# Token mixer of a small audio tower: spectral products with swapped operands, spectra turned through DRAM, inverse transforms in one row

## The reference

```python
B, T, C, HID, K, H = (8, 256, 128, 512, 31, 4)     # x here is (64, 125, 128)
w = jax.nn.softmax(logits, axis=-1)                # 31 taps for each token and head
y = jnp.einsum('bthk,btkhd->bthd', w, xg).reshape(Bq, Tq, Cq)
y = y.transpose(0, 2, 1) + bias[None, :, None]
z = jax.lax.conv_general_dilated(y, Wc, (1,), 'VALID', dimension_numbers=('NCH', 'OIH', 'NCH'))
z = z + bc[None, :, None]
z = jax.nn.selu(z.transpose(0, 2, 1))
return z @ W2.T + b2
```

## Time and profile before

| | us |
|---|---|
| median of three runs | 2085.88 (2084.6 to 2088.66) |
| the profiled execution | 2083.48 |
| its span in the trace | 2081.4 |
| the token mixer in it | 0 to 457.0 |
| its four chunks | 158.1 to 457.0 |
| PE busy, whole span | 1879.5 (90%) |

### The profile page before, as it was taken

One profiled execution on the slowest core, in us unless ns is written; L12 is line 12 of the kernel. 1 busy time (PEld: TensorE's weight loads), 2 busy tenths in 40 slices (PEclk: granted clock), 3 DMA queues, 4 the chain that ended last, 5 costly groups with the idle time before them and its releaser, 6 DMA issues. The chain is left out here.

```text
span 2081.4 us, 46638 instructions
## 1 busy us (share of the span) xinstructions
PE 1879.5 (90%) x16570; PEld 1313.2 (63%) x16570; DVE 1522.3 (73%) x3461; ACT 1257.5 (60%) x2263; POOL 968.1 (47%) x874
## 2 busy tenths in 40 slices
PE   5889999979999799999999999989999999958882
PEld 4678878855555456666666666556666666646771
DVE  5543464446888699999999999657778878867785
ACT  2444464455555377777777777667777777625771
POOL 0000000003454398888888887700344544565773
PEclk9999999999999899999999999999999999959996
DMA  8870010028990000000000000000000000036886
GB/s 295 324 274 20 23 42 11 1 61 361 413 397 5 12 11 11 11 10 10 10 10 10 10 10 10 20 11 2 2 16 19 12 15 20 13 90 194 227 226 209
DMA packets 87385, 178.52 MB, mean 86 GB/s; under 512 B 25917, under 2 KB 63214, under 8 KB 77846
## 3 DMA queue, kind: packets, MB, share of 16 engines
q1 hardware_dynamic: 78646, 160.11, 22.6%
q0 software_dynamic: 6624, 12.70, 1.8%
q10 hardware_dynamic: 1920, 3.11, 0.4%
HBM read 82.00 MB, written 94.86 MB: 85 GB/s over the span
## 5 line engine op out<-in xcount | busy, mean ns | idle before, releaser
L1154 ACT ACTIVATE b_pool_b<-b_pool_a,c_b 128x1024 f32<-128x1024 f32 x384 | 436.6, 1150 | 176.8 <-DVE b_pool_a L1390 154.2
L1227 POOL TENSOR_TENSOR b_pool_c<-b_pool_b 128x512 f32<-128x512 f32 x384 | 491.5, 1288 | 111.2 <-ACT b_pool_b L1154 61.7
L1390 DVE TENSOR_TENSOR b_pool_a<-b_p_s,c_shares 128x1024 f32<-128x1024 f32 x384 | 454.1, 1216 | 50.9 <-PE b_p_s L993 43.7
L991 PE MATMUL b_p_s<-c_x_hi,c_w_hi 128*128 128x512 f32 x384 | 296.3, 772 | 1.9 <-DVE b_pool_a L1390 1.9
L998 PE MATMUL b_p_y<-b_pool_c,c_w 128*128 128x512 f32 x384 | 196.7, 593 | 0.0
L998 PE MATMUL b_p_p<-b_pool_c,c_w 128*128 128x512 f32 x384 | 194.8, 591 | 0.0
L256 POOL COPY a_work<-a_vec 128x64 f32<-128x64 f32 x4 | 1.2, 304 | 378.3 <-PE a_p_A L347 224.6
L1279 DVE TENSOR_TENSOR b_pool_b<-b_p_s,b_decay 96x384 f32<-96x384 f32 x256 | 124.6, 546 | 41.6 <-PE b_p_s L862 41.3
L992 PE MATMUL b_p_s<-c_x_lo,c_w_hi 128*128 128x512 f32 x384 | 153.4, 399 | 0.0
L993 PE MATMUL b_p_s<-c_x_hi,c_w_lo 128*128 128x512 f32 x384 | 152.0, 396 | 0.0
L654 POOL TENSOR_TENSOR d_ln_rstd<-d_ln_var,d_ln_power 128x2 f32<-128x2 f32 x48 | 33.8, 704 | 250.1 <-DVE d_ln_var L650 250.1
(11 more groups left out here) (352 smaller groups left out, 4591.0 us busy)
## 6 DMA issues: line engine op xcount, KB each, us to landing
slots<-b_pool_c SPq DMA_DIRECT2D x55, 1040.0 KB, 25.4
e_wb<-e_weights SPq DMA_DIRECT2D x111, 164.0 KB
band_scratch<-a_work SPq DMA_DIRECT2D x16, 1024.0 KB, 5.6
a_work<-band_scratch SPq DMA_DIRECT2D x16, 1023.5 KB, 8.0
a_raw<-in_Wc SPq DMA_DIRECT2D x16, 512.0 KB, 3.8
e_xb<-slots SPq DMA_DIRECT2D x111, 65.0 KB
c_shares<-c_share_lists SPq DMA_DIRECT2D x12, 512.0 KB, 3.7
e_yb<-e_again SPq DMA_DIRECT2D x12, 512.0 KB, 6.1
```

The costliest lines, as they stand in the source:

```text
L991: nc.tensor.matmul(p_h[q % SLOTS][:, 0:WIDE], w1_hi[:, q, :], x_hi[s][:, :], start=True, stop=False)
L1154: nc.scalar.activation(hid[q % SLOTS][:, :, :], gelu_in[q % SLOTS][:, :, :], ACT.Gelu, bias=b1[:, q:q + 1]).then_inc(s_ge, 1)
L1227: nc.gpsimd.tensor_tensor(both[q % SLOTS][:, :], hid[q % SLOTS][:, 0, :], hid[q % SLOTS][:, 1, :], ALU.add).then_inc(s_bo, 1)
L1390: v.tensor_tensor(gelu_in[q % SLOTS][:, :, :], p_h[q % SLOTS][:, 0:WIDE].unsqueeze(1).to_broadcast([128, 2, WIDE]), shares[s][:, :, :], AL ...
```

## The change

- The two operands of the products are swapped: the piece of `R` is loaded as weights and the piece of `V` moves. A bank then holds (part, example) by (frequency, output channel). Number and size of the matmuls are as before; the first one has 64 columns of weights in place of 64 moving ones.
- The copies of a bank go to one of four buffers `zs[k % 4]`, 256 KB each, and SP writes it from there to a tensor in DRAM, `z_scratch` (two of them, chunks in turn), in pieces of 512 bytes. A copy waits until the write of the bank four earlier has landed.
- SP reads the tensor back by groups of 4 examples, 125 rows (coefficients) of 2 KB, into one of eight buffers `zt[k % 8]`. The first read of a chunk waits for all its writes; a read into a used buffer waits for the `to_time` that used it.
- `turn`, `turned_out` and POOL's copies are gone. The bias comes in as the `bias` operand of ACT's copy out of `p_conv`, which is an ACTIVATE Identity now. `idft` has 125 rows.
- Order on PE: 16 products (with the last two `project` of the chunk before behind the first two), 8 `weights` in a row, then 16 `to_time` with `project` of group g-2 behind each from the third on. On ACT and DVE all copies of a chunk's weights stand in a row behind the products' copies.
- SP: the writes of a chunk, one load of `raw`, eight reads, three loads of `raw`, eight reads.

```diff
@@ product
-                    nc.tensor.matmul(bank[:, cols], V[:, j, :], R[:, f, 0:2 * NB], start=True, stop=False,
-                                     skip_group_check=True)
+                    nc.tensor.matmul(bank[:, cols], R[:, f, 0:2 * NB], V[:, j, :], start=True, stop=False,
+                                     skip_group_check=True)
@@ SP
+            def write_z(o, i):
+                ...
+                sp.wait_ge(s_zs[i % 2], NBK // 2 * o + i // 2 + 1)
+                ...
+                sp.dma_start(spectra[o % 2][first:end, :, :].rearrange("(f r) b o -> (r b) f o", r=2),
+                             z_out[:, 0:(end - first) // 2, :]).then_inc(s_zw[k % ZW], 16)
+
+            def read_z(o, g):
+                k = NG * o + g
+                if g == 0:
+                    for s in range(ZW):
+                        sp.wait_ge(s_zw[s], landed(NBK * (o + 1) - ZW + s))
+                if k >= ZR:
+                    sp.wait_ge(s_cmm, k - ZR + 1)
+                sp.dma_start(zt[k % ZR], spectra[o % 2][:, g * GB:(g + 1) * GB, :]).then_inc(s_zr[k % ZR], 16)
+            for o in range(NO):
+                for i in range(NBK):
+                    write_z(o, i)
+                if o < NO - 1:
+                    load_raw(4 * o + 7)
+                for g in range(ZR):
+                    read_z(o, g)
+                if o < NO - 2:
+                    for i in range(4 * o + 8, 4 * o + 11):
+                        load_raw(i)
+                for g in range(ZR, NG):
+                    read_z(o, g)
@@ PE
-                for g in range(NG):
-                    turn(o, g)
-                    if o < NO - 1 and g % 2 == 0:
-                        weights(CHUNK * (o + 1) + g // 2)
-                    if g > 0:
-                        to_time(o, g - 1)
-                    if g > 1:
-                        project(o, g - 2)
-                to_time(o, NG - 1)
-                project(o, NG - 2)
+                if o < NO - 1:
+                    for v in range(CHUNK):
+                        weights(CHUNK * (o + 1) + v)
+                for g in range(NG):
+                    to_time(o, g)
+                    if g >= 2:
+                        project(o, g - 2)
@@ ACT
+                if k >= ZW:
+                    act.wait_ge(s_zw[k % ZW], landed(k - ZW))
...
-                nc.scalar.copy(zc[g % 2], p_conv[:, 0:N].rearrange("o (n s) -> o n s", n=GB)).then_inc(s_zc, 1)
+                nc.scalar.activation(zc[g % 2], p_conv[:, 0:N].rearrange("o (n s) -> o n s", n=GB), ACT.Identity,
+                                     bias=vecs(o)).then_inc(s_zc, 1)
@@ DVE
-                for g in range(NG):
-                    if o < NO - 1:
-                        weights_out(CHUNK * (o + 1) + g // 2, 2 + g % 2)
-                    if g == 0:
-                        continue
-                    selu(o, g - 1)
-                    if g > 1:
-                        add_h(o, g - 2)
+                if o < NO - 1:
+                    for late in range(CHUNK * (o + 1), CHUNK * (o + 2)):
+                        weights_out(late, 2)
+                        weights_out(late, 3)
+                for g in range(NG):
+                    if g >= 2:
+                        add_h(o, g - 2)
+                    selu(o, g)
```

More of the change, by code:

```diff
@@ L124, in phase_token_mixer @@
         at[0] = 0
-        zs = carve(128, NB, NF2 + 1)
-        zt = [carve(NF2 + 1, GB, 128) for s in range(2)]
+        zs = [carve(128, 4, 128) for s in range(ZW)]
+        zt = [carve(NF2, GB, 128) for s in range(ZR)]
         zc = [carve(128, GB, SP) for s in range(2)]
@@ L147, in phase_token_mixer @@
         s_vmm, s_V = sem("v_product"), [sem("v_copied_act"), sem("v_copied_dve")]
-        s_zmm, s_zs, s_bcz = sem("z_product"), [sem("z_copied_act"), sem("z_copied_dve")], sem("bc_column")
-        s_ztm, s_zt, s_cmm, s_zc, s_ez, s_rz, s_z, s_omm, s_h = (
-            sem("z_turned"), sem("zt_copied"), sem("z_time"), sem("z_copied"), sem("z_exp"), sem("z_relu"), sem("z"), sem("out_product"),
+        s_zmm, s_zs = sem("z_product"), [sem("z_copied_act"), sem("z_copied_dve")]
+        s_zw, s_zr = [sem(f"z_written{s}") for s in range(ZW)], [sem(f"z_read{s}") for s in range(ZR)]
+        s_cmm, s_zc, s_ez, s_rz, s_z, s_omm, s_h = (
+            sem("z_time"), sem("z_copied"), sem("z_exp"), sem("z_relu"), sem("z"), sem("out_product"),
             sem("h"))
@@ L154, in phase_token_mixer @@
         scratch = nc.dram_tensor("band_scratch", (BS * 128 * row,), F32, kind="Internal").ap()
+        spectra = [nc.dram_tensor(f"z_scratch{s}", (NF2, NB, 128), F32, kind="Internal").ap() for s in range(2)]
         def written(s):
@@ L169, in phase_token_mixer, with landed @@
         CHUNK = MPO // PER
+        def landed(k):
+            constant = k // NBK + 1 if k % ZW == 0 else 0
+            return 16 * (k // ZW + 1 + constant)
         def copied(v):
@@ L239, in _ @@
             load_xtok(NG - 1)
-            for i in range(4, NO * MPO // MPC):
-                load_raw(i)
+            def write_z(o, i):
+                k = NBK * o + i
+                first, end = BANKS[i]
+                z_out = zs[k % ZW]
+                sp.wait_ge(s_zs[i % 2], NBK // 2 * o + i // 2 + 1)
+                if i == 0:
+                    sp.dma_start(spectra[o % 2][0, :, :], z_out[0:NB, 0, :]).then_inc(s_zw[k % ZW], 16)
+                    first, z_out = 1, z_out[:, 1:4, :]
+                sp.dma_start(spectra[o % 2][first:end, :, :].rearrange("(f r) b o -> (r b) f o", r=2),
[8 more added lines that the diff above has]
+                sp.dma_start(zt[k % ZR], spectra[o % 2][:, g * GB:(g + 1) * GB, :]).then_inc(s_zr[k % ZR], 16)
+            for i in range(4, 7):
+                load_raw(i)
+            for o in range(NO):
[10 more added lines that the diff above has]
+                    read_z(o, g)
         FIRST, DFT, LATE = 16 * 3, 16 * 2, 16 * 4
@@ L249, in _ @@
             nc.gpsimd.memset(ln_alpha[:, :], math.log(SELU_ALPHA)).then_inc(s_zero, 1)
[L250 to L257, removed]
         @block.tensor
@@ L318, in product @@
                     pe.wait_ge(s_R, NG)
-                    if o > 0:
-                        pe.wait_ge(s_zt, NG * o)
-                if i >= 2:
+                if o > 0 or i >= 2:
                     pe.wait_ge(s_zs[i % 2], NBK // 2 * o + i // 2)
                 bank = p_A[i % 2]
-                j = first
+                j, at = first, 0
                 if j == 0:
-                    last = nc.tensor.matmul(bank[:, 0:NB], V[:, 0, :], R0[:, :], start=True, stop=True,
-                                            skip_group_check=True)
-                    j = 1
@@ L329, in product @@
-                while j < end:
-                    f, cols = j // 2, slice((j - first) * NB, (j - first + 2) * NB)
-                    nc.tensor.matmul(bank[:, cols], V[:, j, :], R[:, f, 0:2 * NB], start=True, stop=False,
-                                     skip_group_check=True)
-                    last = nc.tensor.matmul(bank[:, cols], V[:, j + 1, :], R[:, f, NB:3 * NB], start=False, stop=True,
-                                            skip_group_check=True)
-                    j += 2
@@ L336, in product @@
-                last.then_inc(s_zmm, 1)
-            def turn(o, g):
-                k = NG * o + g
-                if g == 0:
[L341 to L349, removed]
+                    nc.tensor.matmul(bank[0:NB, 0:128], R0[:, :], V[:, 0, :], start=True, stop=True, skip_group_check=True)
@@ new lines, in product @@
+                    j, at = 1, 128
+                while j < end:
+                    f, cols = j // 2, slice(at, at + 128)
+                    nc.tensor.matmul(bank[:, cols], R[:, f, 0:2 * NB], V[:, j, :], start=True, stop=False,
+                                     skip_group_check=True)
+                    last = nc.tensor.matmul(bank[:, cols], R[:, f, NB:3 * NB], V[:, j + 1, :], start=False, stop=True,
+                                            skip_group_check=True)
+                    j, at = j + 2, at + 128
@@ L356, in to_time @@
                 for n in range(GB):
-                    last = nc.tensor.matmul(p_conv[:, n * SP:(n + 1) * SP], zt[g % 2][:, n, :], idft[:, :],
+                    last = nc.tensor.matmul(p_conv[:, n * SP:(n + 1) * SP], zt[k % ZR][:, n, :], idft[:, :],
                                             start=True, stop=True, skip_group_check=True)
@@ L439, in z_out @@
                 first, end = BANKS[i]
[L440 to L451, removed]
+                k = NBK * o + i
+                act.wait_ge(s_zmm, k + 1)
+                if k >= ZW:
+                    act.wait_ge(s_zw[k % ZW], landed(k - ZW))
+                z_out, bank = zs[k % ZW], p_A[0][:, :].rearrange("p (f o) -> p f o", o=128)
+                pairs = slice(0, (end - first) // 2)
+                if i == 0:
+                    nc.scalar.copy(z_out[0:NB, 0, :], bank[0:NB, 0, :])
```

(41 more changed lines are left out.)

10 lines of the change are left out of this document (6 added, 4 removed).

## The result

The changed kernel takes 2122.16 us (median of four runs, 2120.36 to 2122.98) against 2085.24 of the kernel before beside it: 1.0174 times as long (95% interval 1.0162 to 1.0187), 36.9 us more. Forecast were 2128 us and a range of 2094 to 2144. In the profiled execution (span 2118.4) the token mixer's chunks go from 157.40 to 494.7, 337.3 us, where they took 298.9 before. All ratios in this document are of executions in the chip's usual state; one execution of a later kernel, the one with three extra matmuls in each wait, took 6356 us and is in none of them.

The account below looks back on a forecast made before the run. PE was taken to bound product and inverse stretches; 10.3 us at the upper clock plus 32.1 for the falling clock made 42.4 on the 2085.9 median, about 2128 us, range 2094 to 2144.

Parts of the forecast that it names:

- Products: Product stretches: matmuls unchanged, copies hidden, one `project` more (0.72 us) in chunks 2 to 4, a 0.70 us wait gone in three.
- Writes: Writes of 256 KB to DRAM land in about 4 us, hidden while under about 5.9; far bound 10.2.
- The rival of late writes: Writes to DRAM landing at 9 us add 50 us, giving 2150 to 2180 us; chance 0.05.
- Weights in a row: Eight `weights` behind a chunk's products: period 2.73 us, 20.2 us a row, where they cost PE 8.8 before.
- Inverse in a row: `to_time` waits for ACT's copy out of single bank `p_conv`: 1.89 us a group, next product at 30.2 us.
- Reads: Reads back from DRAM: hidden in chunks 1 to 3; last chunk's first `to_time` 6.7 us behind its products.
- The other pace of reads: Reads of 125 rows on 5 engines: some 2 us each instead of 0.7, last chunk ending some 2 us later.
- The rival that PE sets this pace: Inverse part at 1.69 us a group, set by PE's own work: 2083.4 us, not slower; chance 0.05.
- The clock: PE's clock falls in three rows of `weights` and the last chunk's wait: 32.1 us together, bounds 0 and 50.
- The rival that it holds: PE's clock stays up in the rows of `weights`, only the last chunk's wait makes it cold: 2098 us; chance 0.17.
- The sum: All four chunks: 10.3 us more at the upper clock plus 32.1 for the clock, 42.4 us.
- the first case: PE's clock falls: 2128 us, own range 2106 to 2145 from the cold stretches' two bounds; chance 0.72.

Follow-up runs that it names:

- the extra matmuls: Changed kernel plus six unneeded 128x128x128 matmuls on PE behind each of a chunk's first seven `weights`: ratio 1.0051 to the kernel before, chunks 313.3 us.
- the second bank: Changed kernel with a second PSUM bank for `to_time`, odd groups in `p_A1`: ratio 1.0099 to the kernel before, chunks 321.6 us.
- split reads: Kernel with three `weights` before the first `to_time`, five spread, each 125-row read split into 112 and 13 rows: ratio 0.9952 to the kernel before.
- the kernel with three `weights` ahead: Changed kernel with three of a chunk's eight `weights` before the first `to_time`, five spread over later groups: ratio 1.0012 to the kernel before, chunks 302.7 us.

## Why the prediction was right

- **What bounds.** PE, as read from the earlier trace rows. It bound the changed kernel's products too; in the rows of `weights` the wait for DVE's copies set the pace, as forecast.
- **Products.** 29.85 and 29.54 us against 29.7 and 29.4: right.
- **Writes.** They land in 2.3 us (median of 56 of 256 KB; the longest took 4.5), where I took 4 and had 10.2 as the far bound: hidden, right, and less than the nearest row said. The rival of late writes, which decides from 5.9 us on, falls.
- **Weights in a row.** A period of 2.64 us against 2.73, and 3.55 at the lower clock: right. With the extra matmuls, at the upper clock, a row takes 19.6 us; 20.2 were forecast.
- **Inverse in a row.** 1.87 us a group against 1.89, with ACT's copy with bias at 0.58 as the row said, and the second bank shows the cause. The rival that PE sets this pace falls.
- **Reads.** Hidden in chunks 1 to 3 of the changed kernel, as forecast. The last chunk's first `to_time` came 7.31 us behind the products, not 6.7. The other pace of reads, about 2 us each, was left as a side case and kept out of the sum, and it was the true one. It cost 1.6 us in that wait (5.7 with split reads), where the side case had said some 2; the last chunk's term came near only because its 6.7 was 1.0 too long for quick reads, which is luck. Elsewhere the pace did no harm as long as PE was slower, and cost some 3 us more in the kernel with three `weights` ahead.
- **The clock.** It fell in all three rows and in the last wait. Behind two `weights` in chunks 1 and 2, as taken; behind four in chunk 3. The rival that it holds falls by the trace: with holes of 1.47 us behind 1.17 of work the clock fell. The Trainium skill (TensorE: Matmul & The Clock Gate, Loop structure matters more than you think) has copies by another engine leave PE's warmth alone in a loop whose next matmuls follow at once; here they had to wait for the copies, so the rule doesn't carry over to a row of such steps.
- **The sum.** By chunk 88.4, 88.1, 86.2 and 74.6 us against 89.5, 89.2, 89.2 and 73.4. The mis-sized terms are the row and the inverse part of chunk 3 (2.5 us too much, since two `weights` more ran at the upper clock, and 0.7; its products took 0.1 more), the same two in chunks 1 and 2 (1.1 each), and, the other way, the last chunk's wait (0.6) and its products and inverse part (0.6 together). That makes 38.4 us in the chunks against 42.4. The first product started 0.7 us earlier; over all traces that start scatters from 157.4 to 160.6. So the token mixer ends 37.7 us later, and the medians differ by 36.9. One bound doesn't fit the working: the first case's own range begins at 2106, but with no cold stretch, the lower bound that it names, the sum is 2096.
- **Split of the loss.** In chunks 1 to 3 the clock is 23 to 24 us of it, shown by the extra matmuls; 28.2 were forecast. Of the remaining 14, 5.2 are the last chunk's (74.6 us against 69.4), which had no extra matmuls and started cold; how much of it the clock is (3.9 forecast) no run shows by itself. The other 9 are the holes and the single bank less the 16 turns of a chunk (10.2 forecast). I argued that from the rows, and the second bank shows 14.5 us of what could be had back, but no run kept the turns beside this order.

## What to carry to other kernels

Work taken off the engine that bounds is worth nothing if the same edit takes away what lay beside its waits: put the removed work and the newly uncovered waits into one sum. Steps that hand over through a single buffer should stand among other work, not in a row. And where the matmul engine would stand still in every one of many short steps, as here for 1.47 us in every 2.64, don't count on the upper clock: price its later work at the lower one, or fill the waits with matmuls that nobody needs. A turn through DRAM takes work off the engine only if something else covers the way there and back, here 7.3 us a chunk.

## What I had not expected of the hardware

- Three extra matmuls of 0.22 us in every hole (0.6 us of standing still in 2.64) held the clock as well as six did.
- A load of 125 rows used about 5 of the 16 DMA engines (share 0.33, 124 GB/s), the same rows as one load of 112 and one of 13 used 14 of them (0.90, 270 GB/s).
- A write of 256 KB to DRAM in pieces of 512 B landed in 2.3 us, sooner than a load of the same size in a busy stretch (3.2).
